# A graph network's attention stage on one core: a block's maximum is found later in the step order, and links and gaps share four partitions

## The reference

```python
q = (xn @ Wq + bq).reshape(n, H, DH)
k = (xn @ Wk + bk).reshape(n, H, DH)
v = (xn @ Wv + bv).reshape(n, H, DH)
ep = ef @ We + be
scores = jnp.einsum('ehd,ehd->eh', q[dst], k[src] + ep[:, None, :]) * scale
scores = scores * ew[:, None]
m = jax.ops.segment_max(scores, dst, num_segments=n)
ex = jnp.exp(scores - m[dst])
s = jax.ops.segment_sum(ex, dst, num_segments=n)
attn = ex / s[dst]
out = jax.ops.segment_sum(attn[:, :, None] * v[src], dst, num_segments=n)
```

## Time and profile before

| | us |
|---|---|
| median of 3 runs | 7592.93 |
| lowest and highest run | 7581.71, 7601.85 |
| the profiled execution | 7604.27 |
| its span, first to last instruction | 7602.6 |
| `att_edges`, about 5330 to 7152 | 1822 |

### The profile page before, as it was taken

How to read it: one execution, slowest core, us unless ns; L and a number is a source line. 1 busy time by engine, 2 the same in 40 slices (tenths; PEclk the granted TensorE clock), 3 DMA queues, 4 the chain that set the end, 5 groups by cost and what they waited for, 6 DMA issues and landing times. The chain is left out here.

```text
span 7602.6 us, 102739 instructions
## 1 busy us (share of the span) xinstructions
PE 4797.7 (63%) x17972; PEld 3531.7 (46%) x17973; DVE 4400.3 (58%) x10687; ACT 2860.9 (38%) x8083; POOL 4327.5 (57%) x3848
## 2 busy tenths in 40 slices
PE   6366666623444444575566565548587777787799
PEld 4244334412222222354444444435466666666688
DVE  3366666684555555584444444456577777776654
ACT  0133333334545554432222222212355555555543
POOL 1666666605555565437888888853566666665310
PEclk8666776666666666797777777779788888887899
DMA  6344443334555554316777777764555555555210
GB/s 217 106 109 109 107 106 105 105 97 145 155 151 157 155 158 147 112 51 104 104 104 104 103 105 104 103 151 157 157 160 156 159 154 158 160 160 146 78 34 28
DMA packets 677825, 946.82 MB, mean 125 GB/s; under 512 B 105024, under 2 KB 532928, under 8 KB 677505
## 3 DMA queue, kind: packets, MB, share of 16 engines
q0 software_dynamic: 279840, 593.16, 34.4%
q1 hardware_dynamic: 371938, 324.51, 14.6%
q10 hardware_dynamic: 25728, 26.21, 1.0%
HBM read 761.16 MB, written 182.33 MB: 124 GB/s over the span
## 5 line engine op out<-in xcount | busy, mean ns | idle before, releaser
L1619 POOL DMA_INDIRECT gcn<-c_update,c_target x832 | 1320.6, 1587 | 276.4 <-issue 215.9
L1256 PE MATMUL psum<-g_rows,g_onehot 128*128 128x256 f32 x1664 | 671.3, 553 | 918.5 <-issue 591.1
L1171 POOL DMA_INDIRECT g_rows<-x,g_idx x832 | 824.8, 991 | 589.7 <-PE psum L1256 292.2
L663 POOL DMA_INDIRECT e_rows<-hrow,e_idx x832 | 813.8, 978 | 489.0 <-issue 240.2
L1987 POOL DMA_INDIRECT s_rows<-kv,s_idx x832 | 820.9, 987 | 318.3 <-issue 217.4
L1256 PEld LDWEIGHTS psum<-g_rows,g_onehot 128*128 128x128 f32 x1664 | 408.1, 267 | 1181.7 <-issue 741.2
L726 PE MATMUL psum<-e_rows,e_onehot 128*128 128x265 f32 x1664 | 661.8, 552 | 314.2 <-issue 140.4
L1567 PE MATMUL psum<-c_same,c_onehot 128*128 128x128 f32 x1664 | 360.8, 384 | 638.7 <-DVEq L1545 638.7
L1239 DVE SCALAR_TENSOR_TENSOR g_run<-g_run,keep,psum 128x256 f32<-128x256 f32 x832 | 398.2, 479 | 609.7 <-issue 373.7
L1567 PEld LDWEIGHTS psum<-c_same,c_onehot 128*128 128x128 f32 x1664 | 305.8, 275 | 742.3 <-DVEq L1545 420.6
L2074 PE MATMUL psum<-queries_sums,s_spread 128*128 x1664 | 574.2, 505 | 100.8 <-issue 74.7
(11 more groups left out here) (358 smaller groups left out, 9424.0 us busy)
## 6 DMA issues: line engine op xcount, KB each, us to landing
g_attr<-in_edge_attr SPq DMA_DIRECT2D x832, 128.0 KB
c_srow<-rows_src SPq DMA_DIRECT2D x208, 256.0 KB
e_drow<-rows_dloc SPq DMA_DIRECT2D x208, 128.0 KB
s_drow<-rows_dloc SPq DMA_DIRECT2D x208, 128.0 KB
s_feat<-in_edge_feat SPq DMA_DIRECT2D x832, 32.0 KB
gcn<-p_zero ACTq DMA_DIRECT2D x8, 3200.0 KB
n_sums<-gcn SPq DMA_DIRECT2D x100, 256.0 KB
x<-n_out POOLq DMA_DIRECT2D x75, 256.0 KB
```

The source lines that it names most:

```text
L663: pool.indirect_dma_start(rows[u][:, s, 0:D + H], None, k.hrow, bass.IndirectOffsetOnAxis(ap=idx[u][:, s:s + 1], axis=0)).then_inc(gathere ...
L1171: pool.indirect_dma_start(rows[q][:, s, :], None, k.x1, bass.IndirectOffsetOnAxis(ap=idx[q // RING][:, at:at + 1], axis=0)).then_inc(gathe ...
L1256: pe.matmul(k.psum[:, s, 0:D], onehot[b][:, s, :], rows[q][:, s, :], start=True, stop=True).then_inc(summed, 1)
L1619: pool.indirect_dma_start(k.gcn[a], bass.IndirectOffsetOnAxis(ap=target[q][:, a:a + 1], axis=0), update[q][:, a, :], None, compute_op=ALU. ...
```

## The change

WEIGH, SUM and ADD grow by one group of steps; the exponentials come in step q = 2 of ACT. On DVE `find_top` and `below_top` move behind the reduction and the third sum of step q = 1; the copy of the last link becomes `carry_on`, behind `times_query`; `take_ends` and `link_steps` come later in step q = 0. `far` and `gap` become two halves of one tile of four partitions, so that one product reads both, and `select` has four rows and four matrices; the setup of DVE has 17 counted instructions in place of 12.

```diff
-    WEIGH, SUM, ADD = 5, 6, 7
+    WEIGH, SUM, ADD = 6, 7, 8
-    SETUP = 12
+    SETUP = 17
-        join, far = sb("s3_join", [2, H, T]), sb("s3_far", [2, H, T])
-        gap = sb("s3_gap", [2, H, SB])
-        select = sb("s3_select", [2, 3, P])
-        is_first = sb("s3_is_first", [2, 1])
+        join, far_gap = sb("s3_join", [2, H, T]), sb("s3_far_gap", [4, H, T])
+        far, gap = far_gap[0:2], far_gap[2:4]
+        select = sb("s3_select", [4, 4, P])
+        is_row = sb("s3_is_row", [4, 4])
...
-                    if q == 1 and block_before(n, 1).live:
+                    if q == 2 and block_before(n, 1).live:
                         expo(block_before(n, 1))
...
-                pe.matmul(fwd, select[:, 0, :], far[:, :, 0:SB], start=True, stop=False)
-                pe.matmul(fwd, select[:, 0, :], gap[:], start=False, stop=False)
+                pe.matmul(fwd, select[:, 0, :], far_gap[:, :, 0:SB], start=True, stop=False)
                 pe.matmul(fwd, ident16[:], wide(k.first_gap), start=False, stop=True)
-                pe.matmul(back, select[:, 1, :], far[:, ::-1, SB - 1::-1], start=True, stop=False)
-                pe.matmul(back, select[:, 1, :], gap[:, ::-1, ::-1], start=False, stop=False)
+                pe.matmul(back, select[:, 1, :], far_gap[:, ::-1, SB - 1::-1], start=True, stop=False)
                 pe.matmul(back, ident16[:], wide(k.last_gap), start=False, stop=True)
-                pe.matmul(link[:, 0:H], select[:, 0, :], far[:, :, 0], start=True, stop=False)
-                pe.matmul(link[:, 0:H], select[:, 2, :], far[:, ::-1, SB], start=False, stop=True
+                pe.matmul(link[:, 0:H], select[:, 2, :], far_gap[:, :, 0], start=True, stop=False)
+                pe.matmul(link[:, 0:H], select[:, 3, :], far_gap[:, ::-1, SB], start=False, stop=True
...
+            def carry_on(at):
+                dve.tensor_copy(far[0:1, :, 0], far[0:1, :, SB]).then_inc(far_chain, 1)
+
             def take_ends(at):
-                dve.tensor_copy(far[0:1, :, 0], far[0:1, :, SB]).then_inc(far_chain, 1)
                 dve.wait_ge(ends_ready, at.n + 1)
...
-                    if q == 1 and done.live:
-                        find_top(done)
                     if at.live:
                         add_features(at)
-                    if q == 1 and done.live:
-                        below_top(done)
                     if q == 0 and done.live:
                         scan_on(done)
...
                     if at.live:
                         times_query(at)
+                    if q == 0 and done.live:
+                        carry_on(done)
                     add_step(sums, 1, j)
                     if at.live:
                         reduce_heads(at)
+                    if q == 1 and done.live:
+                        find_top(done)
+                    add_step(sums, 2, j)
                     if q == 0 and done.live:
                         take_ends(done)
-                    add_step(sums, 2, j)
-                    if q == 0 and done.live:
-                        link_steps(done)
+                    if q == 1 and done.live:
+                        below_top(done)
                     if q == GB - 1 and at.live:
                         finish_logits(at)
                     if Group(n, q, 2).live:
                         spread_group(Group(n, q, 2))
+                    if q == 0 and done.live:
+                        link_steps(done)
                     add_step(sums, 3, j)
```

More of the change, by code:

```diff
@@ L2138, in _ @@
             ch.tick(dve.memset(join[:], -BIG))
-            ch.tick(dve.memset(far[:], -BIG))
+            ch.tick(dve.memset(far_gap[:], -BIG))
             ch.tick(dve.memset(local[:], 0.0))
@@ L2142, in _ @@
             ch.tick(dve.tensor_copy(ident16[:], k.ident[:]))
-            ch.then(dve.tensor_scalar(is_first[:], k.lane[0:2, :], -1.0, 1.0, ALU.mult, ALU.add))
-            ch.tick(dve.tensor_scalar(select[:, 0, :], k.iota[0:2, :], 0.0, is_first[:, 0:1], ALU.mult, ALU.add))
-            ch.then(dve.tensor_scalar(select[:, 1, :], k.iota[0:2, :], 0.0, k.lane[0:2, 0:1], ALU.mult, ALU.add))
-            ch.then(dve.tensor_scalar(select[:, 2, :], select[:, 1, :], -1.0, None, ALU.mult))
+            for a in range(4):
+                ch.tick(dve.tensor_scalar(is_row[:, a:a + 1], k.lane[0:4, :], float(a), None, ALU.is_equal))
+            ch.wait()
+            ch.tick(dve.tensor_scalar(select[:, 2, :], k.iota[0:4, :], 0.0, is_row[:, 0:1], ALU.mult, ALU.add))
+            ch.then(dve.tensor_scalar(select[:, 3, :], k.iota[0:4, :], 0.0, is_row[:, 1:2], ALU.mult, ALU.add))
+            ch.tick(dve.tensor_scalar(select[:, 0, :], select[:, 2, :], is_row[:, 2:3], None, ALU.add))
+            ch.then(dve.tensor_scalar(select[:, 1, :], select[:, 3, :], is_row[:, 3:4], None, ALU.add))
+            ch.then(dve.tensor_scalar(select[:, 3, :], select[:, 3, :], -1.0, None, ALU.mult))
             assert ch.n == SETUP
```

## The result

The changed kernel takes 7499.84 us (median of 4 runs, 7490.50 to 7517.66) against 7597.39 us for the kernel before in runs beside it: ratio 0.9867, 95% interval 0.9824 to 0.9909, or 98 us gained. The forecast was 7402 us, a gain of 191 us, with a range up to 7485 us: the sign was right, the size was half, and the result lies outside the range. Two later comparisons on one other chip gave 0.9850 (0.9831 to 0.9870) and 0.9852 (0.9825 to 0.9879).

The account below looks back on a forecast made before the run. Waits between engines bound the stage, chiefly DVE's before the maximum. -254 (maximum) - 50 (sums) + 27 (loop edge) + 31 (rescale) + 52 (overlaps) + 3 (setup, drain) = -191 us: 7402 us, range 7335 to 7485.

Parts of the forecast that it names:

- The maximum moves: DVE's 254.0 us wait before the maximum goes; in plain blocks the hand-back ends at +7.45, DVE asks at +9.3.
- Sums: DVE's wait before the sums: 50 of 74.7 us gone, since step q=2's sums come at full clock; ends 0 and 75.
- to the first sums of q=1: Rival: PE waits for weighing, POOL for the ring, or the delayed hand-back moves the wait there; 7593 us, chance 0.04.
- Loop edge and rescale: Wait left at the maximum: 27 us at the edge of the three-block loop, 31 us from rescale lengthening PE's gap before ends.
- Overlaps: POOL's weighing lengthens DVE instructions through the shared port pair: one overlap per block at 1.0 us, 52 us added.
- the slower rival: POOL blocks DVE at the end of every step, 1.55 us per hit; four hits a block give 7672 us, chance 0.04.
- POOL, ACT, SP, the links: POOL (25.1 us a block) does not bound, its ACT wait mostly goes; SP issues nothing new; four-partition products cost no more.
- Setup and drain: Five more DVE setup instructions, 1 to 2 us, and the last group summed a step later, 0 to 4 us: together 3.
- PE keeps its low clock: Rival: the gap ahead of ends and loop-edge stalls keep PE's clock low, sums' waits stay, more overlaps; 7511 us, chance 0.14.
- the level expected for the forecast: Sign: PE's granted clock in the stage rises from 0.80 to about 0.85.

Follow-up runs that it names:

- short weighing: Changed kernel, POOL multiplying one column per head in place of 32: 7530.23 us, ratio 0.9857, on the first kind of chip; 6678.08 us, 0.9599, on the other.
- reordered kernel: Changed kernel, scan_back ahead of rescale and first sum, edge features' products ahead of ends at q=0: 7432.41 us, 0.9786; other kind of chip 6730.18 us, 0.9661.

## Why the prediction was wrong in size

**The maximum moves: right in kind, with luck in the size.** 254.0 us became 2.6, where the sum left 58 us (27 at the loop edge, 31 for rescale). Neither stayed at the maximum. But the margin is thin: the hand-back ends 11.1 us behind scan_back's start, in plain blocks and behind the edge alike, where +7.45 was forecast for the plain ones (the kernel before has 9.1 on average, and the block that was read 8.06). DVE asks at +11.4, not +9.3, since it has waited at q=1's sum and been held by POOL first. The maximum is in time because DVE is late too.

**Sums: this term failed.** "With no idle PE after the hand-back, step q=2's sums come at full clock", 50 us less. They do come at full clock (6321.32, 1.94 us; that stretch has a granted clock of 0.99), so the wait that the low clock made there is gone, and DVE waits for them all the same: 1.75 us a block, where it was 1.07. With 0.96 at q=1, where there was none, and some 0.6 at q=0 and q=3, this makes about the 166.6 us, +92. Two causes are shown. The waits can be shared out between them, what each is worth in time only in part.
- *Order.* ends never starts before scan_back has ended, and the gap ahead of it, read as 1.41 us and forecast as 2.0, was 3.7 us in plain blocks and 6.5 behind the loop edge (before: 1.7 and 4.5, averaged over the middle of the stage, 5560 to 6900 us). PE then starts q=0 late, the hand-back pushes q=1's look-up and sums, and the sums of q=1 wait 0.96 us a block. With scan_back first that wait is 0.2 and 0.4 us. Not all of the longer gap is order: with short weighing it is 3.2 us in plain blocks on the first kind of chip and 1.97 on the other. By the two comparisons on one chip each this is 31 or 68 us of the missing 93. The prediction had priced rescale's delay only as a leftover at the maximum; it named the shift "to the first sums of q=1" as a rival at 0.04 and did not give its mechanism a share of the forecast.
- *PE's late signals.* The wait at q=2, about 91 us in the stage, is of this kind: DVE starts 1.98 us behind the end of the products, where 0.25 is usual. Summing DVE's idle time by step over the same blocks (4940 to 6180 us on the other chip), the short-weighing kernel waits before q=2's first sum 1.29 us a block on a chip of the first kind and 0.15 on the other; before scan_on 0.90 and 0.17; before take_ends' copy 0.67 and 0.0. But before q=1's first sum 1.10 and 0.90: that one is order, on either chip. That 1.97 us of the other kind of chip is the 2.0 of the forecast, but without POOL's full weighing. Whether the whole forecast would have held there is open.

**Loop edge and rescale (+58).** Their lateness exists (above) but was paid at the sums, so it is in the +92.

**Overlaps (+52): nearly right in length, wrong as a price.** scan_back +14 us, the copy +20, link_steps +8, spread +19, rescale's two +8, finish_logits -1: 68 us of longer instructions, 61 in DVE's busy time. Instructions over 0.25 us longer than the shortest of their line were 14 before and are 54 now, one per block, as forecast. The overlap's length of 1.5 to 1.8 us (6308.88) is that of the earlier trace rows. In the change, on the first kind of chip, they cost nothing that can be measured: take them away, and DVE waits for PE instead. In the reordered kernel on the other kind, where DVE is busy 1389 of 1548 us of the stage, they cost 85 us. Kernel and kind of chip differ together here, so which of the two decides is not shown.

The lock that the Trainium skill states (SBUF — State Buffer, "SBUF: two separate sides") fits the rows in part. All 54 instructions ended 0.03 to 0.30 us behind the end of a weighing, even a copy of 8 values. But by that section the instruction that starts first has the ports and the other waits, and 49 of the 54 have a start ahead of the weighing's. The profile's spans on POOL are rough, so these rows can't show who was first. The price in the slower rival, every hit paid in full in the kernel's time, did not hold.

**POOL, ACT, SP, the links: right.** POOL did not bound and changed its wait as said. Four-partition products cost what two-partition ones did (L2107: 0.48 us both), and with them alone nothing was gained.

**Setup and drain (+3):** the stage began 16 us later, which two profiles' earlier stages differ by anyway; no term of it can be read.

**The rivals.** "PE keeps its low clock" forecast 7511 us, close to the measured 7500, for a wrong reason: the clock rose from 0.80 to 0.84, the level expected for the forecast. A number that fits does not show its mechanism.

The kernel with scan_back ahead of rescale beats the kernel before and the change: 0.976 and 0.981 of the kernel before, and with the edge features' products first 0.979 and, on the other kind of chip, 0.966.

## What to carry to other kernels

When a wait of one engine goes, list every signal that engine gives later in the same step, and which engine runs dry until then: here scan_back should have moved ahead of the work that moved in. While an engine stands at a wait, the others catch up; price its removal by the next wait of each, not by its length. And measure the cost of longer instructions by taking them away, in the kernel and on the kind of chip that count. In the change on one chip 61 us of DVE's busy time were worth nothing; in the reordered kernel on another 92 us were worth 85.

## What was not expected of the hardware

PE's signals came late against the ends that the profile gives its products: 2.5 us in the block shown, to DVE, ACT and POOL together, at a granted clock of 1.00. Ahead of scan_on, which started up to 4.4 us behind the transpose's end in the change, they did so in 16 to 19 of its 52 blocks in all three profiles, and in 0 or 1 of 52 for four kernels of the new order on one other chip. On that chip the kernel before took 6965 us, against 7597 to 7639 on the others; most of the difference lies ahead of this stage, which there began some 600 us earlier. What holds the signals back, and whether PE truly works longer than the profile's ends say, wasn't found.
